# Four stacked graph layers on one core: the node tables of the first layer move from a phase of their own into the edge phase

## The reference

```python
past, future = (edge_index[0], edge_index[1])
x_past, x_future = x[past], x[future]
fwd_in = jnp.concatenate([x_future, x_past, edge_attr], axis=1)
flow_fwd = _mlp(fwd_in, W1f, b1f, W2f, b2f)
fwd_agg = jax.ops.segment_sum(flow_fwd, future, num_segments=x.shape[0])
bwd_in = jnp.concatenate([x_past, x_future, edge_attr], axis=1)
flow_bwd = _mlp(bwd_in, W1b, b1b, W2b, b2b)
...
x = _layernorm(x + _L0_gnn_ref(...), axis=-1)
```

## Time and profile before

| | |
|---|---|
| median of 3 runs | 3043.38 us (3042.61 to 3052.16) |
| the profiled execution | 3040.35 us, of which the span from first to last instruction is 3037.9 us |
| PE, DVE, ACT, POOL busy | 78%, 65%, 32%, 48% of the span |
| load phase, first to last instruction | 814.46 to 867.68 us |
| edge phase of layer 0, first instruction | 868.28 us; first matmul at 888.76 us |

### The profile page before, as it was taken

How to read it: one execution, slowest core, us unless ns; L and a number is a source line. 1 busy time by engine, 2 the same in 40 slices (tenths; PEclk the granted TensorE clock), 3 DMA queues, 4 the chain that set the end, 5 groups by cost and what they waited for, 6 DMA issues and landing times. The chain is left out here.

```text
span 3037.9 us, 72809 instructions
## 1 busy us (share of the span) xinstructions
PE 2359.2 (78%) x27993; PEld 1700.1 (56%) x27993; DVE 1976.0 (65%) x5117; ACT 965.9 (32%) x1879; POOL 1470.1 (48%) x1845
## 2 busy tenths in 40 slices
PE   0538877999159999999999735888888759996696
PEld 0213333333038888888888523555555549995574
DVE  5815444444179999999999635999899835443001
ACT  1014333333015555555555312444344300000010
POOL 2017777777515555555555225999899800000000
PEclk9957666555569999999999857999999969997897
DMA  8954444444203333334334267555555330003955
GB/s 358 367 221 115 114 113 113 114 113 111 78 19 110 110 126 137 110 116 147 110 109 153 92 155 183 144 150 147 145 145 150 97 77 3 3 3 123 419 242 244
DMA packets 251426, 424.06 MB, mean 140 GB/s; under 512 B 127586, under 2 KB 213244, under 8 KB 241747
## 3 DMA queue, kind: packets, MB, share of 16 engines
q1 hardware_dynamic: 195124, 334.25, 31.4%
q0 software_dynamic: 54800, 83.75, 11.0%
q10 hardware_dynamic: 1164, 1.37, 0.1%
HBM read 229.60 MB, written 209.72 MB: 145 GB/s over the span
## 5 line engine op out<-in xcount | busy, mean ns | idle before, releaser
L331 POOL DMA_INDIRECT sorted_edges<-s_records,s_index x400 | 476.3, 1191 | 312.8 <-issue 308.3
L1529 PE MATMUL m_p_acc<-m_prod,m_oh 128*128 128x344 f32 x1250 | 412.2, 474 | 17.7 <-issue 17.3
L1083 DVE TENSOR_SCALAR e_ohw<-e_iota,e_rec 128x128 bf16<-128x128 f32 x628 | 400.2, 696 | 0.0
L867 POOL TENSOR_TENSOR e_ohw<-e_oh,e_rec 128x512 bf16<-128x512 bf16 x314 | 332.3, 1078 | 76.0 <-DVE e_oh L1075 76.0
L1529 PEld LDWEIGHTS m_p_acc<-m_prod,m_oh 128*128 128x128 f32 x1250 | 232.9, 196 | 121.4 <-issue 31.5
L873 POOL TENSOR_TENSOR e_part<-e_rest,e_part 128x256 bf16<-128x256 f32 x157 | 103.7, 660 | 401.1 <-ACT e_part L903 395.1
L1432 POOL TENSOR_SCALAR m_oh<-m_iota,m_rec 128x128 f32<-128x128 f32 x314 | 264.4, 852 | 0.1
L1786 PE MATMUL q_p_next<-q_g,A 128*128 128x96 bf16 x5250 | 224.8, 206 | 0.0
L1786 PEld LDWEIGHTS q_p_next<-q_g,A 128*128 128x128 bf16 x5250 | 223.7, 98 | 0.0
L1097 DVE COPY e_strip<-e_p_aw 128x512 f32<-128x512 f32 (+1 forms) x325 | 199.9, 656 | 1.4 <-PE e_p_aw L975 1.2
L1576 DVE TENSOR_TENSOR m_prod<-m_rec,m_coef 128x256 f32<-128x256 f32 x471 | 198.4, 472 | 0.0
(11 more groups left out here) (346 smaller groups left out, 4883.8 us busy)
## 6 DMA issues: line engine op xcount, KB each, us to landing
dense_strips<-e_strip SPq DMA_DIRECT2D x25, 3200.0 KB, 11.1
r_W<-dense_strips SPq DMA_DIRECT2D x47, 1600.0 KB, 24.7
m_rec<-sorted_edges SPq DMA_DIRECT2D x138, 526.0 KB, 3.8
sorted_edges<-s_neg SPq DMA_DIRECT2D x5, 12560.0 KB, 68.2
A<-dense_strips POOLq DMA_DIRECT2D x25, 800.0 KB, 24.4
e_rec<-sorted_edges SPq DMA_DIRECT2D x156, 108.0 KB, 2.2
sorted_edges<-s_records,s_index POOLq DMA_INDIRECT x400, 3.9
m_rec<-sorted_edges SPq DMA_DIRECT2D x12, 394.5 KB, 3.4
```

The lines of the kernel that those rows point to most:

```text
L331: pool.indirect_dma_start(dram["edges"], bass.IndirectOffsetOnAxis(ap=index[u % RING][:, c:c + 1], axis=0), record[u % RING][:, c, :], Non ...
L867: i = g_.tensor_tensor(ohw[g % 4][:, :, k, :], oh[s][:, :, 0, :], rec[s][:, :, c:c + 1].to_broadcast([P, G, P]), ALU.mult)
L1083: i = V.tensor_scalar(ohw[g % 4][:, t, 0, :], iota[:, :], rec[s][:, t, CSRC:CSRC + 1], rec[s][:, t, CW:CW + 1], ALU.is_equal, ALU.mult)
L1529: i = mm(p_acc[d % 2][:, 0:TERMS], oh[g % 4][:, t % G, :], prod[g % 3][:, t % G, :], start=(t % NB == 0), stop=(t % NB == NB - 1), skip_gr ...
```

## The change

`load_nodes_phase` and its barrier and `clear` are removed. The edge phase makes the tables at the head of its own instruction lists:

- The host hands in the features already transposed and padded (`x_turned`, 32 x 3200), so that one DMA fills `xT`, and the transposes and the copies of L652 and L664 are gone.
- A step makes the tables of two blocks (13 steps, the last with one block). Its products go to one of three PSUM banks that the pipeline uses only later (`p_hid`, `p_aw0`, `p_aw1`).
- The four parts of a split are spread: ScalarE writes the high part and the middle part, VectorE the rest (in one of two buffers `tab_rest`), GpSimd the low part. ScalarE takes the high part of a step ahead of the middle part of the step before.
- `x` itself is loaded behind the records' first eight loads, and SyncE waits for it ahead of the nine small DMAs.

```diff
-def load_nodes_phase(nc, io, keep):
...
+        TABLES = -(-NB // 2)
+        p_tab = [p_hid[:, :], p_aw[0][:, :, :].rearrange("p a c -> p (a c)"), p_aw[1][:, :, :].rearrange("p a c -> p (a c)")]
...
+        def table(i):
+
+            n = min(2, NB - 2 * i)
+            return n, tab[:, 2 * i:2 * i + n, :, :], p_tab[i % 3][:, 0:n * 4 * H1].rearrange("p (b c) -> p b c", b=n)
...
         @block.sync
         def _(sp):
+            sp.dma_start(xT[:, :], io["x_turned"]).then_inc(n_load, 16)
+            for k, part in enumerate((io["L0_gnn_W1f"][D:2 * D, :], io["L0_gnn_W1b"][0:D, :], io["L0_gnn_W1f"][0:D, :], io["L0_gnn_W1b"][D:2 * D, :])):
+                sp.dma_start(wsd[:, k, :], part).then_inc(n_load, 16)
             sp.dma_start(iota[:, :], io["sort_consts"][:, 1, :]).then_inc(d_const, 16)
+            sp.dma_start(ident[:, :], io["sort_consts"][:, 0, :]).then_inc(d_const, 16)
...
             for g in range(2, U):
                 load(g)
+            sp.wait_ge(cleared, 1)
+            sp.dma_start(x[0:NL, :, :], io["x"].rearrange("(p b) f -> p b f", b=NB)).then_inc(n_x, 16)
+            sp.wait_ge(n_x, 16)
             sp.wait_ge(w_chain, 4)
...
         @block.gpsimd
         def _(pool):
             g_ = nc.gpsimd
+            for i in range(TABLES):
+                n, to, _ = table(i)
+                tab_mid.after(pool, i)
+                tab_low.set_by(g_.tensor_tensor(to[:, :, 2, :], tab_rest[i % 2][:, 0:n, :], to[:, :, 1, :], ALU.subtract))
...
         @block.scalar
         def _(act):
+            for i in range(TABLES + 1):
+                if i < TABLES:
+                    n, to, y = table(i)
+                    tabled.after(act, i)
+                    tab_hi.set_by(nc.scalar.copy(to[:, :, 0, :], y))
+                if i:
+                    n, to, _ = table(i - 1)
+                    tab_cut.after(act, i - 1)
+                    tab_mid.set_by(nc.scalar.copy(to[:, :, 1, :], tab_rest[(i - 1) % 2][:, 0:n, :]))
...
         @block.tensor
         def _(pe):
             mm = nc.tensor.matmul
+            pe.wait_ge(n_load, 80)
+            for i in range(TABLES):
+                n, _, y = table(i)
+                tab_cut.before(pe, i, 3)
+                for k in range(n):
+                    m = mm(y[:, k, :], xT[:, (2 * i + k) * P:(2 * i + k + 1) * P], wsd[:, :, :].rearrange("p k h -> p (k h)"), start=True, stop=True,
+                           skip_group_check=True)
+                tabled.set_by(m)
             pe.wait_ge(d_b, 288)
...
             def hidden(g):
                 s = g % 2
+                if g == 0:
+                    tab_low.after(pe, TABLES - 1)
...
         @block.vector
         def _(dve):
             V = nc.vector
+            V.memset(x[:, :, :], 0.0).then_inc(cleared, 1)
             V.memset(w2[:, :, :], 0.0)
             V.memset(ones3[:, :], 1.0).then_inc(setup, 1)
+            for i in range(TABLES):
+                n, to, y = table(i)
+                tab_hi.after(dve, i)
+                tab_low.before(dve, i, 2)
+                dve.sem_inc(prime, 1)
+                tab_cut.set_by(V.tensor_tensor(tab_rest[i % 2][:, 0:n, :], y, to[:, :, 0, :], ALU.subtract))
```

80 lines of the change are left out of this document (13 added, 67 removed).

## The result

| | before | after |
|---|---|---|
| median of the runs side by side | 3043.02 us (3042.61 to 3052.16, 4 runs) | 3022.57 us (3020.27 to 3024.88, 4 runs) |
| the profiled execution | 3040.35 us | 3020.27 us, span 3018.4 |

The ratio is 0.9936, with a 95% interval of 0.9911 to 0.9961: faster by 0.6%, 20 us. The forecast was 3007.1 us in 3000 to 3017, so it was wrong by 15.5 us. The changed kernel was timed in two more groups, where it came out at 0.991 and 0.9906. Over the three groups the gain is 20 to 28 us, where 36 was forecast.

The account below looks back on a forecast made before the run. VectorE's pace in the load phase, then 20.5 us without a matmul, were taken to delay the pipeline. Moving its start from 888.76 to 852.5 us saves 36.3: 3004.1 us against the profiled execution, 3007.1 for the median, range 3000 to 3017.

Parts of the forecast that it names:

- What bounds the kernel now: Load phase and edge phase's head: VectorE sets the tables' pace; the change is worth what it moves TensorE's start, 888.76 us.
- Arrival of the features: Head of the edge phase: the transposed features land and the tables can start at 819.0 us (818.3 to 821.5).
- The rival of late features: Few DMA engines carry the 32 long rows; TensorE starts 8 to 9 us later, 3016 us; chance 0.09, shared with `x`.
- Rate of the tables: Table steps of two blocks each, at the head of the edge phase: 1.5 us a step on average.
- The first rival: TensorE stays at half clock in the tables: 2.0 us a step, time 3012.1 us; chance 0.18.
- the ring of 1.4 us: Two `tab_rest` buffers in the tables: subtraction, middle copy, low subtraction and hand-overs, 2.8 us for two steps.
- End of the tables: VectorE's last table subtraction ends at 841.0 us, after 22 us of tables.
- From there to the start: VectorE's preparation, cuts and nine small DMAs behind the tables: TensorE starts the pipeline at 852.5 us.
- The sum: TensorE's start of the edge pipeline moves from 888.76 to 852.5 us, 36.3 us less.
- the GpSimd rival: VectorE slows GpSimd's table subtraction to 2.03 us, a step takes 1.8 us, time 3011 us; chance 0.08.
- The slower rival: Edge pipeline partly at half clock: 72 us of it use up the gain, 100 give 3057 us; chance 0.03, with no change.

Follow-up runs that it names:

- free80_none: Changed kernel with spare increments at the end of TensorE's sort list and no tables made, VectorE filling the table with zeros: 3002.72 us, ratio 0.9864.

## Why the prediction was wrong

**The step that failed** is the end of "What bounds the kernel now": "it needs the same instructions in either kernel. So the change is worth just what it moves TensorE's start of the pipeline, 888.76 us." The start moved nearly as forecast; what was gained there didn't reach the end. The same instructions didn't take the same time when they lay elsewhere in the code. Shown: the loop of the second layer had a second gap behind each jump back and took about 10 us more (289.0 to 289.9 in three traces against 280.7 and 278.1). 80 instructions that do nothing brought it back to 280.8 and the time to 3007.7, and 176 of them gave the kernel before the same second gaps (a loop of 289.5 us in two traces, 281.1 in a third) and a longer time without anything else of the change. That the gaps are code being fetched fits the packets and the shift by 38 instructions for 40, but it is inferred from them.

**Arrival of the features.** Forecast 819.0 (818.3 to 821.5), measured 819.62. The number is near, the path was another. The sort ended sooner in this execution (first issue at 813.85, not 814.46), so from issue to use it was 5.8 us where 4.5 was forecast. The features landed 3.8 us behind their issue, at about 817.7, and the first matmul waited for the last weight load. The prediction took 1.5 us for the landing of a small load; behind the large one it was 3.7. The rival of late features didn't occur.

**Rate of the tables.** Forecast 1.5 us a step, measured 1.71. The first rival was what happened, half clock throughout, and its chance of 0.18 was too low. Its price, 2.0 us, was too high: 8 records in 3.62 us are 1.8 a step, overlapping a little. I had argued that without gaps the clock would rise, as behind the transposes; the transposes ("128*32") have 128 rows in use. The Trainium skill, "TensorE: Matmul & The Clock Gate", Part 1, says that the clock is set by how busy TensorE has been. The trace doesn't agree if busy is read as the profile's busy time: 91% at 32 rows had the half clock and 75% at 128 rows the full one. The swing of the clock that the Trainium skill, "TensorE: Matmul & The Clock Gate", section "A second HAM failure mode: psum-queue depth-cycling", describes didn't occur: TensorE had no idle time between groups, and the clock never swung. With 128 rows the ring of 1.4 us was measured at 1.36. GpSimd's subtraction took 1.15 us (1.2 was taken), never 2.0, so that rival fell too.

**End of the tables.** Forecast 841.0, measured 843.38: 0.6 us from the later first matmul, the rest, 23.8 us of tables instead of 22, from the half clock.

**From there to the start.** Forecast 11.5 us, measured 11.26. The small loads' wait and the load of `x` were hidden as worked out. The cover is the tables: free80_none shows what `x` costs without it. (By its own numbers the prediction's landing of `x` is 836.3, not 836.6.)

**The sum.** Forecast 36.3 us, measured at the start 34.1 (32.6 and 35.6 in two further traces). The missing 2.1 are 1.2 us of the weight loads' landing and 1.8 of the half clock, less 0.2 behind the tables and less 0.6 by which the sort ended sooner. Of 34.1, about 9 went to the loop's second gaps. In the first pair of traces 4 more went to the pipeline, which is within what one kernel shows against itself. Some 1 us lies in smaller differences of the other phases that I didn't follow up.

**Smaller slips.** The prediction reads the eleventh slice of the page as the load phase. It reaches from 759 to 835 us, and most of it is the end of the sort, before the phase begins at 814.46; most of the phase lies in the twelfth, where VectorE has a 7. The price of the GpSimd rival is 11 x 0.3 = 3.3 us, not 3.6.

**The slower rival** put the loss in the pipeline's clock. A lower clock was part of the loss, 5.7 us of slower matmuls in the loop, but in another phase, behind gaps that only the place of the code had brought.

## What to carry to other kernels

When a change adds or removes instructions ahead of a loop that is run several times, look at the gaps named "issue" behind the loop's jump, before and after: they are a part of the result that says nothing of the change, and spare instructions in a wait tell it apart. That TensorE is busy doesn't show that its clock is full: a burst on 32 or 64 rows stayed at the half clock here, so price such a burst from rows at half. A small load issued behind a large one can land as late as the large one; take its landing from a row where it stands behind one. And when tables or other setup stand in front of a pipeline, it is what stands behind them, small serial loads and constants, that can still be moved under them.

## What the runs showed of the hardware

- Code came in packets of 16.4 KB in the mean. After each jump back in a loop of 1250 matmuls a round, TensorE stood 2.8 to 3.4 us, and with some placements a second time for 0.2 to 2.5 us, 8 to 28 matmuls behind the jump. It went on 5.4 to 6.4 us behind the jump then.
- Table matmuls of float32 with 32 or 64 rows kept the granted clock at half with TensorE busy over 90%; with 128 rows, 96 of them zeros, it rose and stayed, though TensorE was busy 75%.
- An increment of a semaphore in TensorE's list took about 0.154 us (96 more of them took 14.8 us).
- A load of 8 KB landed 3.7 us behind its issue where it was issued behind one of 400 KB, and 1.6 us where it wasn't.
- Executions of one kernel differed by up to 20 us in later groups (before: 3030.1 to 3049.4 in 23 runs). Single executions of it can't show a difference of 0.3%; the intervals of five rounds, 0.1 to 0.2% to either side, can.
